# A perceiver layer's self attention: score products in pairs on two halves of the partitions, softmax denominators out of the product with the values, and a new order of the work

## What is computed

```
qkv = x @ ternary(w_qkv).T          # 16 query heads, 4 key/value heads of 16
q, k = rms_norm(q), rms_norm(k);  q, k = rope(q), rope(k);  q = q * gain
scores = einsum('bqhgd,bkhd->bhgqk', q, k) / 4, causal
y = softmax(scores) @ v
x = x + rms_norm(y) @ ternary(w_proj).T
```

## Time and profile before

| | |
|---|---|
| three runs, median | 603.84 us (603.35, 603.84, 603.91) |
| the profiled execution | 601.56 us, its span 599.6 us |
| mean granted TensorE clock | 0.948 |
| busy, PE / DVE / ACT / POOL | 530.7 / 442.6 / 425.3 / 321.0 us |
| share of the span | 89% / 74% / 71% / 54% |

### The profile page before, as it was taken

How to read it: one execution, slowest core, us unless ns; L and a number is a source line. 1 busy time by engine, 2 the same in 40 slices (tenths; PEclk the granted TensorE clock), 3 DMA queues, 4 the chain that set the end, 5 groups by cost and what they waited for, 6 DMA issues and landing times. The chain is left out here.

```text
span 599.6 us, 22296 instructions
## 1 busy us (share of the span) xinstructions
PE 530.7 (89%) x6950; PEld 441.8 (74%) x6950; DVE 442.6 (74%) x1389; ACT 425.3 (71%) x1207; POOL 321.0 (54%) x489
## 2 busy tenths in 40 slices
...
GB/s 247 207 56 61 127 25 124 20 56 92 64 83 70 48 103 13 138 0 109 42 91 62 81 70 57 94 18 134 0 111 40 95 57 82 11 39 0 21 9 10
DMA packets 42743, 41.53 MB, mean 69 GB/s; under 512 B 16080, under 2 KB 33488, under 8 KB 42704
## 3 DMA queue, kind: packets, MB, share of 16 engines
...
...
## 5 line engine op out<-in xcount | busy, mean ns | idle before, releaser
L709 ACT ACTIVATE pr<-sm,nb 128x257 f32<-128x257 f32 x256 | 128.8, 506 | 24.1 <-DVE nb L948 23.8
L497 POOL TENSOR_TENSOR cTl<-cx,cTh 128x516 fp32r<-128x516 f32 x64 | 86.5, 1351 | 108.9 <-ACT cTh L609 108.9
L948 DVE CUSTOM_DVE_ANT_0 sm<-x_ps,mbias 128x257 f32<-128x257 f32 x256 | 99.7, 420 | 36.2 <-PE x_ps L1252 34.3
L609 ACT ACTIVATE pt<-x_ps 128x512 f32<-128x512 f32 x112 | 66.6, 595 | 23.8 <-PE x_ps L1262 23.6
L1262 PE MATMUL x_ps<-tab,pr 128*128 128x128 f32 x512 | 72.5, 278 | 2.1 <-ACT pr L709 1.5
L1144 PE MATMUL x_ps<-cTh,wkTh 128*128 128x258 f32 x256 | 63.5, 330 | 4.5 <-DVE xnTl L804 3.0
L1262 PEld LDWEIGHTS x_ps<-tab,pr 128*128 128x128 f32 x512 | 56.8, 141 | 8.6 <-ACT pr L709 2.7
L506 POOL TENSOR_TENSOR sr<-sv,halfneg 128x20 f32<-128x20 f32 x16 | 56.7, 3542 | 1.3
L1144 PE MATMUL x_ps<-wvTh,cTh 128*128 128x256 f32 x256 | 57.0, 304 | 0.1
L1252 PE MATMUL x_ps<-kk,qbd 32*64 32x257 f32 x1024 | 44.8, 403 | 11.0 <-issue 5.3
L609 ACT ACTIVATE kk<-x_ps 128x257 f32<-128x257 f32 x128 | 48.6, 382 | 5.6 <-PE x_ps L1144 5.6
...
## 6 DMA issues: line engine op xcount, KB each, us to landing
...
```

The lines of the kernel that those rows point to most:

```text
L497: g.tensor_tensor(cxbuf(cT[1], b)[:, :, :], cx[:, b % BT, :, :], cxbuf(cT[0], b)[:, :, :].bitcast(F32), ALU.subtract).then_inc(A_ctl, 1)
L609: return sc.activation(dst, src, ACT.Copy)
L709: sc.activation(pr[:, b % 2, gr, :], sm[:, b % 2, gr, :], ACT.Exp, bias=nb[:, n:n + 1], scale=-1.0, accum_out=st[:, 0, b, gr:gr + 1]).then ...
L948: v.tensor_tensor_reduce(out=sm[:, b % 2, gr, :], in0=xb(f"S{b}", gr)[:, 0:LK], in1=mbias[:, b, :], scale=1.0, scalar=0.1 * NEG, op0=ALU.a ...
```

## The change

The transposes of q and k put two of the four sequences on partitions 0 to 63 and the other two on 64 to 127, by plain fp32 products with halves of the identity in place of transposes. qTs and kbd are [128, 2, ...] for [64, 4, ...]. The four score products go in pairs on the two halves of the rows, each half into a bank of its own (D_S has two banks), and the causal sum is two instructions. The softmax isn't divided by its sum before the product with the values: each head's values get a 17th column of ones (written once ahead of the loop by POOL), so that the product's 17th column is the denominator. D_dn and D_p3 go; D_ys on DVE takes the reciprocals of the 17th columns and multiplies while it moves the result to ys; ACT squares ys. All five orders and the banks are written anew; of the new `BANK` these matter: B_xT 2, B_qkv 2, K 3 1 4, C_hT 3, D_yT 1, PT 2 1 1, D_S 0 and 1.

```diff
     "pe": [
-        ("S", 0), ("B_st",), ("C_xT",), ("K", 1, 0), ("K", 1, 1), ("B_O",), ("V", 1), ("D_kT",), ("PT", 0, 0),
-        ("PT", 0, 1), ("B_oT",), ("S", 1), ("D_QT",), ("K", 2, 0), ("B_wo",), ("K", 2, 1), ("FS", 0), ("PV", 0),
-        ("S", 2), ("D_S",), ("PT", 1, 0), ("V", 2), ("FS", 1), ("C_z", 0), ("B_xT",), ("PT", 1, 1), ("K", 3, 0),
-        ("TT", 0), ("FS", 2), ("K", 3, 1), ("B_qkv",), ("S", 3), ("C_z", 1), ("GATE",), ("C_z", 2), ("PV", 1),
-        ("Q_h",), ("V", 3), ("TT", 1), ("TT", 2), ("D_PV",), ("K", 4, 0), ("D_yT",), ("PT", 2, 0), ("PT", 2, 1),
-        ("C_hT",), ("Q_q",), ("D_pj",), ("C_y",), ("PV", 2), ("TT", 3), ("K", 4, 1), ("PT", 3, 0), ("PT", 3, 1),
-        ("V", 4), ("PV", 3),
+        ("C_xT",), ("S", 0), ("K", 1, 0), ("B_st",), ("B_O",), ("K", 1, 1), ("V", 1), ("D_kT",), ("B_oT",),
+        ("S", 1), ("PT", 0, 0), ("D_QT",), ("B_wo",), ("PT", 0, 1), ("K", 2, 0), ("FS", 0), ("K", 2, 1), ("D_S",),
+        ("C_z", 0), ("PT", 1, 0), ("PV", 0), ("TT", 0), ("TT", 1), ("FS", 1), ("B_xT",), ("S", 2), ("V", 2),
+        ("TT", 2), ("FS", 2), ("K", 3, 0), ("K", 3, 1), ("B_qkv",), ("S", 3), ("C_z", 1), ("GATE",), ("C_z", 2),
+        ("K", 4, 0), ("D_PV",), ("PT", 1, 1), ("Q_h",), ("V", 3), ("D_yT",), ("TT", 3), ("PT", 2, 0), ("PV", 1),
+        ("C_hT",), ("PT", 2, 1), ("D_pj",), ("C_y",), ("Q_q",), ("PV", 2), ("K", 4, 1), ("PT", 3, 0),
+        ("PT", 3, 1), ("V", 4), ("PV", 3),
     ],
     "act": [
-        ("C_xT",), ("CT", 2), ("K", 1, 0), ("T", 0), ("EXP", 0, 0), ("EXP", 0, 1), ("EXP", 0, 2), ("EXP", 0, 3),
-        ("K", 1, 1), ("V", 1), ("PT", 0, 0), ("B_oT",), ("CT", 3), ("PT", 0, 1), ("EXP", 1, 0), ("D_QT",),
-        ("K", 2, 0), ("EXP", 1, 1), ("F", 0, 0), ("EXP", 1, 2), ("K", 2, 1), ("EXP", 1, 3), ("F", 1, 0),
-        ("EXP", 2, 0), ("PT", 1, 0), ("C_z", 0), ("B_xT",), ("F", 2, 0), ("V", 2), ("D_S",), ("PT", 1, 1),
-        ("TT", 0), ("K", 3, 0), ("K", 3, 1), ("CT", 4), ("B_qkv",), ("EXP", 2, 1), ("F", 0, 1), ("C_z", 1),
-        ("GATE",), ("C_z", 2), ("EXP", 2, 2), ("EXP", 2, 3), ("Q_h",), ("EXP", 3, 0), ("V", 3), ("D_PV",),
-        ("D_yT",), ("TT", 1), ("EXP", 3, 1), ("TT", 2), ("C_hT",), ("EXP", 3, 2), ("PT", 2, 0), ("EXP", 3, 3),
-        ("K", 4, 0), ("Q_q",), ("F", 1, 1), ("PT", 3, 0), ("CT", 5), ("TT", 3), ("PT", 3, 1), ("K", 4, 1),
-        ("V", 4), ("B_keep",), ("F", 2, 1),
+        ("C_xT",), ("CT", 2), ("T", 0), ("K", 1, 0), ("EXP", 0, 0), ("EXP", 0, 1), ("K", 1, 1), ("EXP", 0, 2),
+        ("EXP", 0, 3), ("B_oT",), ("V", 1), ("PT", 0, 0), ("EXP", 1, 0), ("D_QT",), ("EXP", 1, 1), ("EXP", 1, 2),
+        ("EXP", 1, 3), ("PT", 0, 1), ("K", 2, 0), ("F", 0, 0), ("C_z", 0), ("K", 2, 1), ("F", 1, 0), ("TT", 0),
+        ("TT", 1), ("PT", 1, 0), ("CT", 3), ("F", 2, 0), ("B_xT",), ("D_S",), ("EXP", 2, 0), ("K", 3, 0),
+        ("CT", 4), ("K", 3, 1), ("V", 2), ("B_qkv",), ("EXP", 2, 1), ("C_z", 1), ("EXP", 2, 2), ("TT", 2),
+        ("F", 0, 1), ("GATE",), ("C_z", 2), ("K", 4, 0), ("EXP", 2, 3), ("PT", 1, 1), ("Q_h",), ("EXP", 3, 0),
+        ("D_yT",), ("D_PV",), ("C_hT",), ("TT", 3), ("EXP", 3, 1), ("EXP", 3, 2), ("PT", 2, 0), ("V", 3),
+        ("EXP", 3, 3), ("F", 1, 1), ("B_keep",), ("CT", 5), ("Q_q",), ("PT", 3, 0), ("PT", 3, 1), ("K", 4, 1),
+        ("F", 2, 1), ("V", 4),
     ],
     "dve": [
-        ("B_comb",), ("S", 0, 0), ("S", 0, 1), ("B_den",), ("B_comb2",), ("S", 0, 2), ("B_o1",), ("S", 0, 3),
-        ("D_scale",), ("T", 0), ("B_O",), ("B_fin",), ("D_kT",), ("S", 1, 0), ("S", 1, 1), ("S", 1, 2),
-        ("S", 1, 3), ("T", 1), ("B_wo",), ("T", 2), ("F", 0, 1), ("B_x1",), ("S", 2, 0), ("S", 2, 1), ("S", 2, 2),
-        ("D_S",), ("T", 3), ("D_mx",), ("B_norm",), ("F", 1, 1), ("F", 2, 1), ("Q_stats",), ("D_s3",), ("C_z", 0),
-        ("F", 2, 3), ("B_xT",), ("C_h", 0), ("S", 2, 3), ("D_dn",), ("Q_norm",), ("D_p3",), ("S", 3, 0),
-        ("B_qkv",), ("S", 3, 1), ("C_z", 1), ("D_p4",), ("C_h", 1), ("C_z", 2), ("C_h", 2), ("C_q", 0),
-        ("C_q", 1), ("S", 3, 2), ("C_q", 2), ("S", 3, 3), ("D_yT",), ("PT", 2, 1), ("C_y",), ("D_pj",),
-        ("D_xstats",), ("D_xq", 0), ("D_xq", 1), ("D_xq", 2),
+        ("B_comb",), ("B_comb2",), ("S", 0, 0), ("S", 0, 1), ("S", 0, 2), ("B_den",), ("B_o1",), ("S", 0, 3),
+        ("T", 0), ("D_scale",), ("B_O",), ("B_fin",), ("D_kT",), ("S", 1, 0), ("S", 1, 1), ("S", 1, 2),
+        ("S", 1, 3), ("T", 1), ("T", 2), ("B_wo",), ("T", 3), ("B_x1",), ("D_S",), ("B_norm",), ("F", 0, 1),
+        ("D_mx",), ("D_s3",), ("F", 1, 1), ("S", 2, 0), ("B_xT",), ("C_z", 0), ("C_h", 0), ("S", 2, 1), ("D_p4",),
+        ("S", 2, 2), ("F", 2, 1), ("F", 2, 3), ("S", 2, 3), ("Q_stats",), ("S", 3, 0), ("S", 3, 1), ("Q_norm",),
+        ("B_qkv",), ("C_z", 1), ("S", 3, 2), ("C_h", 1), ("C_z", 2), ("C_h", 2), ("C_q", 0), ("D_ys",),
+        ("C_q", 1), ("C_q", 2), ("D_yT",), ("S", 3, 3), ("PT", 2, 1), ("C_y",), ("D_pj",), ("D_xstats",),
+        ("D_xq", 0), ("D_xq", 1), ("D_xq", 2),
     ],
     "pool": [
-        ("CL", 2), ("CL", 3), ("D_vbd",), ("PX", 0), ("B_root",), ("Q_root",), ("PX", 1), ("CL", 4),
-        ("B_qkroot",), ("D_yroot",), ("B_rope",), ("PX", 2), ("QBD", 0), ("PX", 3), ("EX",), ("D_xroot",),
-        ("CL", 5), ("QBD", 1), ("QBD", 2), ("QBD", 3),
+        ("CL", 2), ("PX", 0), ("D_vbd",), ("B_root",), ("CL", 3), ("CL", 4), ("Q_root",), ("PX", 1),
+        ("B_qkroot",), ("D_yroot",), ("B_rope",), ("D_xroot",), ("PX", 2), ("CL", 5), ("PX", 3), ("QBD", 0),
+        ("QBD", 1), ("EX",), ("QBD", 2), ("QBD", 3),
     ],
     "sp": [
-        ("LMB", 0), ("LMB", 1), ("LX",), ("LCTX", 0), ("LCTX", 1), ("C_store",), ("LMB", 2), ("LCTX", 2),
-        ("LVX",), ("LCTX", 3), ("LMB", 3), ("LXR",), ("B_shuffle",),
+        ("LX",), ("LCTX", 0), ("LMB", 0), ("LMB", 1), ("LCTX", 1), ("LCTX", 2), ("LMB", 2), ("C_store",),
+        ("LMB", 3), ("LVX",), ("LXR",), ("B_shuffle",), ("LCTX", 3),
     ],
...
-        qTs = sb("qTs", [64, BT, 4, S])
-        kbd = sb("kbd", [64, BT, KV, S])
+        qTs = sb("qTs", [P, 2, 4, S])
+        kbd = sb("kbd", [P, 2, KV, S])
...
-        vbd = sb("vbd", [P, BT * KV, 4, HD])
+        vbd = sb("vbd", [P, BT * KV, 4, HD + 1])
...
+            g.tensor_copy(vbd[:, :, :, HD], m4.unsqueeze(1).to_broadcast([P, BT * KV, 4])).then_inc(W_set, 1)
...
-                            vbd[:, :, :, :],
+                            vbd[:, :, :, 0:HD],
...
-                             xb("D_QT")[0:64, :].rearrange("p (h b q) -> p h b q", h=4, b=BT)).then_inc(B_qTs, 1)
+                             xb("D_QT")[:, 0:D].rearrange("p (h b q) -> p h b q", h=4, b=2)).then_inc(B_qTs, 1)
                     elif k == "D_S":
...
-                            act.wait_ge(B_p3, i1 - 1)
+                            act.wait_ge(B_p4, i1 - 1)
...
                     elif k == "D_PV":
-                        act.wait_ge(B_pv, i1)
-                        if due(i1 - 1):
-                            act.wait_ge(B_yTp, i1 - 1)
-                        copy(ys[:, :], xb("D_PV")[:, 0:D]).then_inc(B_ys, 1)
+                        act.wait_ge(B_ys, i1)
...
-                        sc.activation(ysq[:, :], xb("D_PV")[:, 0:D], ACT.Square, accum_out=yss[:, :]).then_inc(B_yss, 1)
+                        sc.activation(ysq[:, :], ys[:, :], ACT.Square, accum_out=yss[:, :]).then_inc(B_yss, 1)
                     elif k == "D_yT":
...
-                                        xb("D_kT")[0:64, 0:P].rearrange("p (b k) -> p b k", b=BT).unsqueeze(2).to_broadcast([64, BT, KV, S]),
-                                        mj.unsqueeze(1).unsqueeze(3).to_broadcast([64, BT, KV, S]), ALU.mult
+                                        xb("D_kT")[:, 0:2 * S].rearrange("p (b k) -> p b k", b=2).unsqueeze(2).to_broadcast([P, 2, KV, S]),
+                                        mj.unsqueeze(1).unsqueeze(3).to_broadcast([P, 2, KV, S]), ALU.mult
...
                     elif k == "D_S":
...
-                        v.tensor_tensor(s2[:, :, :], xb("D_S")[:, :].rearrange("p (j k) -> p j k", k=S),
-                                        causal.unsqueeze(1).to_broadcast([P, BT * KV, S]), ALU.add).then_inc(B_s2, 1)
+                        for n in range(2):
+                            v.tensor_tensor(s2[:, 8 * n:8 * (n + 1), :], xb("D_S", n)[:, 0:D].rearrange("p (j k) -> p j k", k=S),
+                                            causal.unsqueeze(1).to_broadcast([P, 8, S]), ALU.add).then_inc(B_s2, 1)
                     elif k == "D_mx":
-                        dve.wait_ge(B_s2, i1)
+                        dve.wait_ge(B_s2, 2 * i1)
...
                     elif k == "D_s3":
...
-                    elif k == "D_dn":
+                    elif k == "D_p4":
...
-                        v.tensor_reduce(dn2[:, :], p2[:, :, :], AX.X, ALU.add).then_inc(B_dn, 1)
-                        dve.wait_ge(B_dn, i1)
-                        v.reciprocal(rd2[:, :], dn2[:, :]).then_inc(B_rc2, 1)
-                    elif k == "D_p3":
-                        dve.wait_ge(B_rc2, i1)
```

(42 more changed lines are left out.)

29 lines of the change are left out of this document (15 added, 14 removed), and 7 rows, old and new, of the table BANK.

## The result

The kernel after takes 625.24 us (median of 4; 624.30 to 627.08), the kernel before 603.60 us beside it (4 runs): the ratio is 1.0368, 95% interval 1.0335 to 1.0401. The change makes it slower by 22 us, where the forecast was 600.7 us, 3 us faster, and its range ended at 609.

The account below looks back on a forecast made before the run. PE bounds the middle, a chain of latencies mostly over DVE the drain. Middle +0.8, drain -1.9 and fill -2.0 sum to -3.1 us, set against the median 603.84: 600.7 us, range 593 to 609.

Parts of the forecast that it names:

- rival (d): Score and transpose products: the paired halves run one after the other; +11.8 us, 1 us in the drain, 613.5; chance 0.05.
- The fill: Iteration 0: new order shortens ACT's wait for the first scores of batch 2; -2.0 us, bounds -3.4 and +1.5.
- (7): Drain: iteration 17 gets shorter by -1.9 us, bounds -3 and -0.5; iteration 16 unchanged.
- The short neighbours: PE's new order: groups behind short ones leave issue uncovered; +0.21 us a period, bounds 0 and 0.7.
- rival (c): PE: each change of tiling costs a drain, 26 changes for 21; +9.5 us, 610.2; chance 0.07.
- (6): ACT, POOL and SP: shorter copies and new orders fall into slack; nothing gained or lost.
- rival (b): Chain from S3 through D_ys to C_hT grows and PE stops, C_xT keeping it there; +7.8 us, 608.5; chance 0.14.
- if PE waits at C_xT for kap in the middle: Sign of being wrong in kind: such a wait at the head of PE's iteration in the profile after.
- (5): DVE: -1.06 us of work, worth nothing by itself; chain from S3 to C_hT +0.31 us a period, bounds 0 and +1.0.
- C_xT at the head: PE's order: S0 behind the short C_xT, costed within one more uncovered issue wait of +0.21 us a period.
- The wait for xnTl: PE: K 3 1 no longer shares B_xT's bank, so the wait goes; -0.25 us a period, nothing late next.

Follow-up runs that it names:

- f4: Kernel after with CT 5 and CL 5 moved earlier, S 0 ahead of C_xT on PE and C_xT in bank 0: 602.20 us, ratio 0.9989.
- f3: Kernel after with CT 5 ahead of C_hT on ACT and CL 5 ahead of B_rope on POOL: 610.06 us, ratio 1.0130.
- f1: Kernel before with one ACT step moved, CT 5 ahead of F 1 1 instead of behind PT 3 0: 611.06 us, ratio 1.0145.
- h2: Kernel before with the denominators alone (17th column, D_dn and D_p3 gone, D_ys behind C_q 0): 615.23 us, ratio 1.0200.
- j2: f4 with K 4 1 between D_pj and C_y, PT 2 1 ahead of C_hT, and banks changed to suit: 600.41 us, ratio 0.9959.
- f2: Kernel before with one bank changed, K 3 1 in bank 4 instead of 3: 602.33 us, ratio 0.9989.
- g2: Kernel before with K 3 1 in bank 4 and B_qkv in bank 6 instead of 5: 602.85 us, ratio 0.9998.

## Why the prediction was wrong

**What held.** D_S went from 1.09 to 0.65 us, as said, so the halves do overlap and rival (d) falls. D_QT took 0.62 (0.55 said), D_kT 0.27 where 0.14 was said, D_PV 0.61 for 0.58. The fill gave 3.0 us (2.0 said; which of its steps gave them wasn't traced), iteration 17 1.7 (1.9 said, though the terms of (7) add up to 2.1). The whole drain gave only 0.5, since iteration 15 grew by 1.0, which (7) doesn't cost. The short neighbours: f4, without collision, has a period of 33.19 us, 0.45 over before. Its waits for hb and osc less those gone for xnTl and in front of S 1 make 0.10, the four attention groups make 0; 0.35 is left for the neighbours, for 0.21 taken out of 0 to 0.7. f4 has S 0 back ahead of C_xT, so it has fewer short neighbours than the kernel forecast; even so rival (c)'s extra 0.8 a period has no room in 0.35.

**The step that failed most** stands in (6) and in rival (b): "POOL's D_xroot stands ahead of PX 2, CL 5, PX 3 and QBD 0 now; they are held until DVE's statistics", and "From D_pj to kap's end is 7.01 us ..., and gets Q_q on top ..., about 7.1: even". I asked of POOL's new order only who waits for whom, by semaphores, and not what its instructions do to DVE while they run beside it. In the kernel after D_pj starts at 240.01 and kap ends at 248.09: 8.08 us for 7.01. The difference is xf's 1.10, less 0.15 by which xi and xqb are shorter, and 0.12 ahead of xf. PE's work in between is 6.86 us (7.1 said). So 1.35 us of wait stands where I wrote "even", in nearly every period, and "if PE waits at C_xT for kap in the middle" was my own sign of being wrong in kind. f3 leaves 0.36 of it. The 0.99 us that go in each period, and 1.3 us in each of the three at a lower clock, are the 15 of the 22 us that f3 gives back; f1 puts the same loss, 8 us, into the kernel before. Rival (b) had the right wait, at the right step, and 8 us less than came; it was given 0.14 and the wrong mechanism.

The rows to see it by were there. xf is one of the instructions of which the trace before shows two durations, 0.41 and, once, in the fill, 1.37 us. So is L1007, a VectorE operation with two inputs in SBUF: 0.99 us in the mean of the middle of the kernel before (0.43 at least, 1.57 at most in the whole), where it starts beside POOL's D_vbd and ends 0.28 us after it, and 0.43 us in the kernel after and in f3 and f4. So the old order had such a collision too; what it cost wasn't measured.

**D_ys in the chain.** (5) took +0.31 us for it, bounds 0 and +1.0. It is +0.87 (h2: 8.16 for 7.29), nearly the upper end: I let "some overlap of issue" lower it, while it rose by 0.30 us in which DVE waits, in front of D_ys, for D_PV. What DVE saves by D_dn and D_p3 lies ahead of S 3, where DVE had slack, and is worth nothing, as (5) said; the denominators as a whole cost 12 us (h2). In the kernel after the chain costs PE 0.57 us a period, 0.37 of it at D_PV (its bank 6 is C_z 1's) and 0.20 at C_hT; I had 0.3 to 0.5, all of it at C_hT. How much of the 22 us this chain is stays open: with both waits gone j2's period is only 0.17 us shorter than f4's.

**C_xT at the head.** Costed at one "issue" of 0.21 us; without the collision it is 0.49 a period, and 8 us in all (f3 to f4), 1.7 of them in the drain. 0.36 of the 0.49 is wait that S 0 would have covered; that the rest lies in S 0 behind a short group is argued only.

**The wait for xnTl**, -0.25: f2 and g2 show that at this place 0.2 to 0.35 us are late right behind it. I named B_qkv as three groups away, and didn't look at its bank.
